# Splitting the expert weights to half precision inside the attention loop, with reordered last tile and interleaved expert blocks

## Chip, cores and metric

One core of one Trainium2 chip. The metric is the device time of one launch in microseconds (us), the median of the runs shown. The core has five instruction streams that run beside each other and meet at semaphores: TensorE (PE, with its weight loads PEld), VectorE (DVE), ScalarE (ACT), GpSimd (POOL) and SyncE (SP, which issues most DMAs). The DMAs of all streams share 16 DMA engines.

## What is computed

A graph attention layer over 4096 rows of width 512, then a mixture of 8 experts with the best two for each row. Both add to their input.

```python
def _L0_gnn_ref(query, key, value, adj_matrix, Wq, bq, Wk, bk, Wv, bv, Wm, bm):
    ...
    scores = jnp.einsum('nd,md->nm', q, k) / scale
    adj_scores = scores * adj_matrix
    adj_scores = jnp.where(jnp.abs(adj_scores) < 1e-05, -1000000000.0, adj_scores)
    prob = jax.nn.softmax(adj_scores, axis=-1)
    x = jnp.einsum('nm,md->nd', prob, v)
    return x @ Wm.T + bm
def _L0_ffn_ref(x, Wg, bg, We, be):
    ...
    gate = jax.nn.softmax(x @ Wg + bg, axis=-1)
    topk_vals, topk_idx = jax.lax.top_k(gate, TOP_K)
    ...
    y = jnp.einsum('bsi,eoi->bseo', x, We) + be[None, None, :, :].transpose(0, 1, 2, 3)
    out = jnp.einsum('bseo,bse->bso', y, gate_sparse)
    return out
x = x + _L0_gnn_ref(_layernorm(x, axis=-1), key, value, adj, ...)
x = x + _L0_ffn_ref(_layernorm(x, axis=-1)[None], Wg, bg, We, be)[0]
```

## The kernel before

**Halves of a number.** A product in single precision is made of half-precision ones: each operand is split into a high half (the value rounded to 16 bits, made by ACT) and a low half (what is left, made by DVE), and PE does three matmuls of 128x512 for each 128-deep piece: high by high, high by low, low by high. The helper `product` (L1276) holds these lines (L1280 to L1282), for the scores as for the experts.

**Set-up.** The weights are folded, then queries, keys and values are projected. The keys' and the values' halves stay on chip (`key_region`, `val_region`). The queries' halves go to DRAM (`q_scratch`) and come back one tile of 128 rows at a time into `q_in`, which has one buffer.

**Attention.** 32 tiles (T) of 128 rows, each in 8 chunks (C) of 512 columns. Below, t is the tile whose scores are being made. PE (`attend`, L1400) makes the scores of chunk c (12 matmuls into one of 4 PSUM banks) and, two chunks behind, multiplies the probabilities of tile t-1 by the values (`times_values`, L1372, 12 matmuls into the bank `o_bank`); chunks 6 and 7 of a tile's values come at the start of the next tile. DVE (`attend`, L1142) multiplies a chunk of scores by the adjacency (`times_adj`, L967, which frees its PSUM bank and the adjacency buffer), ACT takes the absolute value (L737), DVE masks and reduces to a maximum (`mask`, L974, L977). After the tile's eighth chunk ACT makes the exponents twice (L745, L750) and DVE their low halves (`low_half`, L989). SP turns each chunk's halves with a DMA transpose (`turn_probs`, L474) into one of four buffers `pT`.

**Routing, inside the same loop.** For tile t-2, DVE adds the residual (L1009), makes the statistics, normalises (L1032), and, from the gate's logits, finds the two best experts and their weights (`route_top2`, `route_gates`, L1055 to L1077, between the mask of chunk 6 and `times_adj` of chunk 7) with one small exponent by ACT in their middle (`gap_exponent`, L784). `route_slots` (L1083 to L1089) gives each row its two places in a DRAM table sorted by expert (`slots`, one table for each half of the rows, 16 tiles each). POOL (L627, L630) scatters the rows into it, one DMA after the other, and then computes the next tile's deviation (L618).

**SP's order** in a tile is written out by hand in `attend_io` (L482) and decides when each DMA is issued: it waits in place for each condition. Its end matters here:

```python
                for c in range(ADJ, C):
                    turn_probs(t - 1, c)
                    if not last:
                        adjacency(t + 1, c - ADJ)
                    if c == 4 and h is not None:
                        turn_rows(t - 2)
                if not last:
                    sp.wait_ge(s_mm, t * C + C)
                    settle()
                    sp.dma_start(q_in, q_dram[t + 1]).then_inc(q_loaded, 16)
```

**Experts' weights.** When the last tile's scores are done, `key_region` is free. Experts' weights come from DRAM in single precision, 1 MB each, through two buffers `we_in` (L527, L532, L796), and are split in halves of an expert by ACT (`expert_hi`, L798, 128x1024) and DVE (`expert_lo`, L1197), 8 of these 16 pieces while the last tile's values are multiplied and 8 among the first expert blocks. The biases (`be`, 2 MB as broadcast) are one DMA of SP (L537).

**Expert blocks.** A half's table has 39 blocks of 128 rows, most real, the last two or three of each half only padding. The 78 blocks run in order, first all of half 0, then all of half 1. Block s is loaded by SP (`load_block`, L547, 8 buffers), turned by PE (`turn_block`, L1430, two blocks ahead), split by ACT (L815) and DVE (L1232), multiplied by PE (12 matmuls), given its bias by DVE (L1240) and its gate weight by ACT (L822), and added into the output by a POOL DMA (L662). `add_block` (L649) waits for the add four blocks back, and, where an expert's run of blocks begins and for each padding block, for all earlier adds to land. Before half 1's blocks can be loaded, SP pads the table's regions (`pad_regions(1)`, L505 to L511) after block 22, and needs the last tile's routing (`route_slots(T - 1)`, `tables(1)`, L1083 to L1133, on DVE after block 9) and POOL's scatters of it.

## Time and profile before

| | |
|---|---|
| runs | 1905.70, 1904.28, 1902.39 us; median 1904.28 us |
| profiled execution | 1899.79 us, of which the instructions span 1898.1 us |
| PE busy | 1817.8 us, 96% of the span |
| DVE, ACT, POOL busy | 1176.2, 730.1, 239.4 us |
| mean granted TensorE clock | 0.981 |
| DMA | 279.67 MB, mean 147 GB/s |
| set-up, attention, experts | about 0 to 245, 245 to 1600, 1600 to 1898 us |

The busy time of PE tells that it is the bound over most of the span. Where something else sets the time is read from what PE waited for and from the chain of work, stage by stage. A start in the rows is in us from the span's start, and the number behind it is the duration. A bracket at a row's end is the engine's idle time before the instruction and what ended it.

### The profile page before, as it was taken

To read this page: it belongs to the slowest core of one execution; us is meant where nothing else is said; L and a number is where in the kernel's file an instruction comes from. 1 tells how busy PE (TensorE), PEld (TensorE's weight loads), DVE (VectorE), ACT (ScalarE), POOL (GpSimd) and SP (SyncE) were. 2 spreads that over 40 slices of the span, in tenths; PEclk is the share of its full clock that TensorE was granted. 3 is DMA by queue.
4 is the path that set the end of the run, shared out by engine and by line. 5 is a ranking of instruction groups with operands and counts; after the bars stand their busy time and mean duration, and the time that the engine had idled before them with its cause. 6 is when DMAs were issued, how large, how long until landed. Compare 5 with 4: busy or idle time off the path is not lost.

```text
span 1898.1 us, 32739 instructions
## 1 busy us (share of the span) xinstructions
PE 1817.8 (96%) x8730; PEld 851.0 (45%) x8731; DVE 1176.2 (62%) x3056; ACT 730.1 (38%) x1381; POOL 239.4 (13%) x277
## 2 busy tenths in 40 slices
PE   8999999999999999999999999999999996789994
PEld 4544444444444444444444444444444443345552
DVE  2788766666666666666666666666666664634542
ACT  1444444443333344433333344433333442433341
POOL 1000000100000000000000000000000010444454
PEclk9999999999999999999999999999999998899997
DMA  5355455555555555555556555555555558788785
GB/s 200 111 177 188 172 136 124 140 142 137 139 138 133 133 133 145 137 142 134 139 128 176 135 135 144 134 145 133 138 133 136 134 137 244 180 194 165 162 161 78
DMA packets 410860, 279.67 MB, mean 147 GB/s; under 512 B 316737, under 2 KB 316737, under 8 KB 410690
## 3 DMA queue, kind: packets, MB, share of 16 engines
q1 hardware_dynamic: 390914, 234.55, 47.8%
q0 software_dynamic: 16736, 38.35, 10.2%
q10 hardware_dynamic: 3168, 6.29, 1.0%
q8 instruction: 16, 0.26, 0.1%
q14 instruction: 26, 0.21, 0.0%
HBM read 144.29 MB, written 59.33 MB: 107 GB/s over the span
## 4 chain that ended last, share of the span: by engine, by line
PE 75%; DVE 8%; DMA 7%; issue 5%; SPq 2%; ACT 2%; DVEq 0%; POOLq 0%; POOL 0%; ACTq 0%
PE ps L1280 16%; PE ps L1282 16%; PE ps L1281 16%; PE ps L1380 8%; PE ps L1381 8%; PE ps L1382 8%; DMA work<-q_scratch 4%; DVE work L967 2%; PE ps L1289 2%; PE ps L1430 1%; ACT work L737 1%; DMA work<-in_WeT 1%; DMA work<-work 1%; PE ps L1327 1%; DVE work L974 1%
## 5 line engine op out<-in xcount | busy, mean ns | idle before, releaser
L1280 PE MATMUL ps<-key_region,work 128*128 128x512 f16 (+1 forms) x1336 | 509.9, 382 | 9.8 <-DMA work<-q_scratch 7.0
L1281 PE MATMUL ps<-key_region,work 128*128 128x512 f16 (+1 forms) x1336 | 509.4, 381 | 0.0
L1282 PE MATMUL ps<-key_region,work 128*128 128x512 f16 (+1 forms) x1336 | 509.2, 381 | 0.0
L1380 PE MATMUL ps<-val_region,work 128*128 128x512 f16 x1024 | 389.6, 380 | 16.3 <-DMA work<-work 11.4
L737 ACT ACTIVATE work<-work 128x512 f32<-128x512 f32 x256 | 161.3, 630 | 597.2 <-DVE work L967 597.1
L1382 PE MATMUL ps<-val_region,work 128*128 128x512 f16 x1024 | 389.6, 380 | 0.0
L1381 PE MATMUL ps<-val_region,work 128*128 128x512 f16 x1024 | 389.5, 380 | 0.0
L967 DVE SCALAR_TENSOR_TENSOR work<-ps,r_cur,work 128x512 f32<-128x512 f32 x256 | 191.8, 749 | 179.0 <-PE ps L1282 163.3
L989 DVE TENSOR_TENSOR work<-work 128x512 f16<-128x512 f32 x256 | 176.4, 689 | 84.0 <-ACT work L750 83.1
L977 DVE CUSTOM_DVE_ANT_0 work<-work 128x512 f32<-128x512 f32 x256 | 177.3, 693 | 51.2 <-DVE work L974 51.0
L1280 PEld LDWEIGHTS ps<-key_region,work 128*128 128x128 f16 x1336 | 131.2, 98 | 172.9 <-issue 28.8
L745 ACT ACTIVATE work<-work,exp_bias 128x512 f32<-128x512 f32 x256 | 181.4, 708 | 65.6 <-DVE exp_bias L985 61.5
L1282 PEld LDWEIGHTS ps<-key_region,work 128*128 128x128 f16 x1336 | 131.4, 98 | 158.8 <-issue 3.4
L1281 PEld LDWEIGHTS ps<-key_region,work 128*128 128x128 f16 x1336 | 131.3, 98 | 148.0 <-issue 3.0
L750 ACT ACTIVATE work<-work,exp_bias 128x512 f16<-128x512 f32 x256 | 180.7, 706 | 0.0
L974 DVE TENSOR_SCALAR work<-work 128x512 f32<-128x512 f32 x256 | 109.2, 426 | 113.2 <-ACT work L737 109.2
L1380 PEld LDWEIGHTS ps<-val_region,work 128*128 128x128 f16 x1024 | 100.2, 98 | 131.8 <-DMA work<-work 12.0
L1382 PEld LDWEIGHTS ps<-val_region,work 128*128 128x128 f16 x1024 | 100.4, 98 | 122.0 <-issue 1.9
L1381 PEld LDWEIGHTS ps<-val_region,work 128*128 128x128 f16 x1024 | 100.4, 98 | 114.0 <-issue 1.5
L662 POOL DMA_INDIRECT out<-val_region,tok_ids x78 | 123.9, 1588 | 152.7 <-DMA out<-val_region,tok_ids 66.6
L627 POOL COPY work<-gate 128x1 f32<-128x1 f32 x64 | 14.6, 228 | 856.9 <-DVE slots_u L1089 776.6
L822 ACT ACTIVATE val_region<-work,tok_gates 128x512 f32<-128x512 f32 x78 | 56.3, 722 | 160.6 <-DVE work L1240 138.8
(149 smaller groups left out, 1542.9 us busy)
## 6 DMA issues: line engine op xcount, KB each, us to landing
work<-in_adj SPq DMA_DIRECT2D x256, 256.0 KB, 2.8
work<-slots SPq DMA_DIRECT2D x40, 257.0 KB
val_region<-slots SPq DMA_DIRECT2D x38, 257.0 KB
work<-in_valueT SPq DMA_DIRECT2D x8, 1024.0 KB, 6.8
work<-in_x SPq DMA_DIRECT2D x8, 1024.0 KB, 5.0
work<-in_keyT SPq DMA_DIRECT2D x8, 1024.0 KB, 5.4
q_scratch<-work SPq DMA_DIRECT2D x8, 1024.0 KB, 5.0
work<-q_scratch SPq DMA_DIRECT2D x32, 256.0 KB, 3.0
```

The costliest lines, as they stand in the source:

```text
L737: nc.scalar.activation(w[:, c * CW:(c + 1) * CW], s_adj[:, c % 2, :], ACT.Abs).then_inc(abs_done, 1)
L745: nc.scalar.activation(prob[:, c % 2, :], w[:, c * CW:(c + 1) * CW], ACT.Exp, bias=exp_bias[:, :], scale=1.0 / SS, accum_out=sum_part[:, c ...
L750: nc.scalar.activation(p_split[:, c, 0:CW], w[:, c * CW:(c + 1) * CW], ACT.Exp, bias=exp_bias[:, :], scale=1.0 / SS).then_inc(p_hi, 1)
L967: nc.vector.scalar_tensor_tensor(s_adj[:, c % 2, :], s_bank(c), r_cur[:, :], adj_in[:, c % ADJ, :], ALU.add, ALU.mult).then_inc(s_read, 1)
L977: nc.vector.tensor_tensor_reduce(out=masked, in0=s_adj[:, c % 2, :], in1=masked, scale=1.0, scalar=-3.0e38, op0=ALU.add, op1=ALU.max, accu ...
L989: nc.vector.tensor_tensor(p_split[:, c, CW:2 * CW], prob[:, c % 2, :], p_split[:, c, 0:CW], ALU.subtract).then_inc(p_lo, 1)
L1280: nc.tensor.matmul(bank, st[0], mv[0], start=(k == 0), stop=False)
L1281: nc.tensor.matmul(bank, st[0], mv[1], start=False, stop=False)
L1282: last = nc.tensor.matmul(bank, st[1], mv[0], start=False, stop=(k == n - 1))
L1380: nc.tensor.matmul(o_bank, st[0], mv[0], start=first, stop=False)
L1381: nc.tensor.matmul(o_bank, st[0], mv[1], start=False, stop=False)
L1382: last = nc.tensor.matmul(o_bank, st[1], mv[0], start=False, stop=final)
```

## The change

**Weights.** In the attention tiles 2 to 17 (the 16 tiles with h == 0), each tile splits a sixteenth of the experts' weights in four pieces of 128x256 values: SP loads a piece (128 KB, rows of 1 KB) into `we_stage`, ACT makes the high half, DVE the low half, and SP stores both (rows of 512 B) in a DRAM scratch `we_halves`. There is one buffer for a piece and one for its halves, so the load of a piece waits for DVE's use of the one before it, and ACT's high half waits for the store of the one before it to have landed. After the last scores ACT issues the loads of the ready halves: experts 0 and 1 at once, expert 2 after the fourth exponent chunk, the other five and all biases (now eight DMAs of 256 KB) after the last exponent. `expert_hi` and `expert_lo` go. SP's `expert_ready` counts experts for PE.

**Last tile.** PE runs its scores in front of most of the values of the tile before (`attend_last`), and its own values go to another PSUM bank (`o_last`), so that they don't wait for the residual of the tile before.

**Blocks.** The first 15 blocks are of half 0; then 48 alternate between the halves; the last 15 are of half 1. Tok buffers go from 8 to 16. The last tile's gate logits come after block 3 (before: 5), its ranks after 6 (8), its slots and tables after 7 (9), its scatters after adds 6 and 8 (10 and 13). The padding of half 1's regions is issued by ACT after block 9, no longer by SP after block 22.

```diff
-    EARLY = 23
-    LATE = 7
+    LEAD = 15
+    AHEAD = 2
+    TOKS = 16
...
-        we = key_region[:, :].rearrange("p (h e k o) -> p h e k o", h=2, e=E, k=KC)
+        we = key_region[:, :].rearrange("p (e h k o) -> p e h k o", h=2, e=E, k=KC)
...
+        we_stage = q1_words[:, 0:WP]
+        we_halves = q1_words[:, WP:2 * WP].bitcast(F16).rearrange("p (h o) -> p h o", h=2)
...
-        weT_v = WeT.rearrange("e (k p) o -> e p k o", p=P)
+        weT_parts = WeT.rearrange("e (a k p) (c o) -> (e a) p k c o", a=2, p=P, c=2)
+        we_dram = nc.dram_tensor("we_halves", (2 * E, P, 2, 2 * D), F16, kind="Internal").ap()
...
+            def __init__(self, first, turn=0, later=False):
+                self.first, self.turn, self.later = first, turn, later
+                middle = LEAD <= first < SEQ - LEAD
+                self.h = (first - LEAD) % 2 if middle else int(first >= LEAD)
+                if middle:
+                    k = (first - LEAD) // 2 + (0 if self.h else LEAD)
+                else:
+                    k = first if first < LEAD else first - BLOCKS
+                at = k + self.h * BLOCKS
+                self.at = at if is0(turn) else at + turn * (TURN // 2)
...
+            def split_piece(i, q):
+
+                if not (is0(i) and q == 0):
+                    sp.wait_ge(piece_lo, i * PIECES + q)
+                settle()
+                sp.dma_start(we_stage, weT_parts[i, :, q // 2, q % 2, :]).then_inc(piece_loaded, 16)
+
+            def store_piece(i, q):
+
+                sp.wait_ge(piece_lo, i * PIECES + q + 1)
+                settle()
+                sp.dma_start(we_dram[i, :, :, q * WP:(q + 1) * WP], we_halves).then_inc(piece_stored, 16)
+
...
+                splits = h == 0
+                if splits:
+                    split_piece(t - 2, 0)
                 turn_probs(t - 1, 0)
                 turn_probs(t - 1, 1)
...
+                if splits:
+                    store_piece(t - 2, 0)
+                    split_piece(t - 2, 1)
                 if h is not None:
...
+                    if splits and c in (5, 6, 7):
+                        store_piece(t - 2, c - 4)
+                        if c < 7:
+                            split_piece(t - 2, c - 3)
                 if not last:
                     sp.wait_ge(s_mm, t * C + C)
                     settle()
                     sp.dma_start(q_in, q_dram[t + 1]).then_inc(q_loaded, 16)
...
-            sp.wait_ge(s_read, T * C)
-            sp.dma_start(we_in[0], weT_v[0]).then_inc(we_loaded[0], 16)
-            for c in range(4):
...
+            for c in range(5):
...
+                if c == 3:
+                    residual_io(T - 2, 1)
...
+            def expert_ready(e):
+
+                sp.wait_ge(we_loaded[e], 48)
+                sp.sem_inc(we_ready, 1)
...
+            for e in range(2, E):
+                expert_ready(e)
+            sp.wait_ge(slotted, 32 * T)
+            sp.wait_ge(padded[1], 16 * E)
+            for st in turn_steps(0):
+                load_block(st)
...
+            def piece_high(i, q):
+                act.wait_ge(piece_loaded, i * (PIECES * 16) + (q + 1) * 16)
+                if not (is0(i) and q == 0):
+                    act.wait_ge(piece_stored, i * (PIECES * 16) + q * 16)
+                nc.scalar.activation(we_halves[:, 0, :], we_stage, ACT.Copy, scale=WS).then_inc(piece_hi, 1)
...
+                    if splits:
+                        piece_high(t - 2, c - 2)
                 if routes:
                     split_rows(t - 2)
                 for c in range(4, 7):
                     absolute(t, c)
+                    if splits and c > 4:
+                        piece_high(t - 2, c - 3)
...
+            def load_expert(e):
+                for a in range(2):
+                    nc.scalar.dma_start(we[:, e, :, 2 * a:2 * a + 2, :].rearrange("p h k o -> p h (k o)"),
+                                        we_dram[2 * e + a]).then_inc(we_loaded[e], 16)
+
+            def load_bias(e):
+                nc.scalar.dma_start(be_all[:, e, :], be[e:e + 1, :].to_broadcast([P, D])).then_inc(we_loaded[e], 16)
+
+            act.wait_ge(piece_stored, 16 * PIECES * 2 * E)
+            act.wait_ge(s_mm, T * C)
+            load_expert(0)
+            load_expert(1)
             for c in range(C):
                 exponent(T - 1, c)
...
+            act.wait_ge(p_hi, T * C)
+            for e in range(3):
+                load_bias(e)
+            for e in range(3, E):
+                load_expert(e)
+                load_bias(e)
...
+                if st.first == 9:
+                    act.wait_ge(tables_done, 2)
+                    for e in range(E):
+                        at = act.value_load(pad_at[0:1, 1, e:e + 1], min_val=0, max_val=(DUMMY - 1) * P)
+                        nc.scalar.dma_start(slots[1][bass.ds(at, P), :], pad_row[:, :]).then_inc(padded[1], 16)
...
+            def piece_low(i, q):
+                dve.wait_ge(piece_hi, i * PIECES + q + 1)
+                nc.vector.scalar_tensor_tensor(we_halves[:, 1, :], we_stage, WS, we_halves[:, 0, :],
+                                               ALU.mult, ALU.subtract).then_inc(piece_lo, 1)
...
                 times_adj(t, 3)
+                if splits:
+                    piece_low(t - 2, 0)
...
                 mask(t, 4)
+                if splits:
+                    piece_low(t - 2, 1)
                 times_adj(t, 5)
                 mask(t, 5)
+                if splits:
+                    piece_low(t - 2, 2)
...
                 times_adj(t, 6)
                 mask(t, 6)
                 if h is not None:
                     route_top2(t - 2)
                     route_gates(t - 2)
+                if splits:
+                    piece_low(t - 2, 3)
                 times_adj(t, 7)
...
-                if c == 0 and not is0(t):
+                if c == 0 and isl(t, T):
+                    pe.wait_ge(s_read, T * C)
+                elif c == 0 and not is0(t):
                     pe.wait_ge(x1_done, t)
...
+            def attend_last():
+
+                t = T - 1
+                scores(t, 0)
+                scores(t, 1)
+                for c in range(C - LAG, C):
+                    times_values(t - 2, c)
+                for c in range(2, 6):
+                    scores(t, c)
+                times_values(t - 1, 0)
+                scores(t, 6)
+                times_values(t - 1, 1)
+                gate_logits(t - 2)
+                scores(t, 7)
+                for c in range(2, C):
+                    times_values(t - 1, c)
+                    if c == 4:
+                        ranks(t - 2)
+
```

## Rows read from the trace of the kernel before

**Rows 1.** Stretches: length, PE, PEld, DVE, ACT, POOL busy, clock, DMA share, GB/s.
```profile
688.00:730.00 42.00, 41.77 (x204) 18.91 (x202) 27.04 (x74) 16.36 (x35) 3.04 (x5) 1.00 0.54 136
1560.00:1602.00 42.00, 28.35 (x126) 12.56 (x125) 21.91 (x52) 16.57 (x26) 4.11 (x5) 0.84 0.93 255
...
1700.00:1866.00 166.00, 166.00 (x876) 89.81 (x875) 81.31 (x216) 65.06 (x108) 77.28 (x51) 1.00 0.84 164
```

**Rows 2.** What PE waited for, whole run: us in total, times, longest.
```profile
PE ps L1280 <- DMA work<-q_scratch: 7.0, 23, 0.5
```

**Rows 3.** PE in order of time, its starts after idle time, from 1576 us.
```profile
1576.27 0.39 PE L1380 MATMUL ps<-val_region,work 128*128 128x512 f16 x1 [2.97 <-DMA work<-work]
1589.05 0.61 PE L1380 MATMUL ps<-val_region,work 128*128 128x512 f16 x1 [8.46 <-DMA work<-work]
1601.52 0.39 PE L1280 MATMUL ps<-key_region,work 128*128 x1 [0.41 <-issue]
...
1658.99 0.68 PE L1430 MATMUL ps<-ident,val_region 128*128 128x128 f32 x4 [2.83 <-DVE work L1232]
```

**Rows 4.** DVE in order of time in one attention tile, chunks 6 and 7.
```profile
657.34 0.75 DVE L967 SCALAR_TENSOR_TENSOR work<-ps,r_cur,work 128x512 f32<-128x512 f32 x1 [2.33 <-PE ps L1282]
...
663.38 0.75 DVE L967 SCALAR_TENSOR_TENSOR work<-ps,r_cur,work 128x512 f32<-128x512 f32 x1 [0.20 <-DVE picked L1077]
```

**Rows 5.** ACT in the same tile, the routing's exponent.
```profile
661.72 0.20 ACT L784 ACTIVATE egap<-gap 128x1 f32<-128x1 f32 x1 [2.89 <-DVE gap L1065]
```

**Rows 6.** SP's DMA issues in the same tile, in order of time.
```profile
653.14 0.34 SPq L465 DMA_DIRECT2D work<-in_adj  x1
...
658.32 0.33 SPq L465 DMA_DIRECT2D work<-in_adj  x1
...
664.36 0.34 SPq L465 DMA_DIRECT2D work<-in_adj  x1
665.02 0.33 SPq L503 DMA_DIRECT2D work<-q_scratch  x1
```

**Rows 7.** PE at the start of the next tile.
```profile
668.20 0.39 PE L1280 MATMUL ps<-key_region,work 128*128 128x512 f16 x1 [0.29 <-DMA work<-q_scratch]
```

**Rows 8.** Line L465, 250 to 1000 us, its DMAs of 256 KB.
```profile
DMA to landing us min/median/max: 2.6/2.8/4.0
```

**Rows 9.** DVE's groups, 1550 to 1660 us: count, busy us, mean ns, idle before.
```profile
L1197 DVE SCALAR_TENSOR_TENSOR key_region<-work,key_region 128x1024 f16<-128x1024 f32 x16 | 19.6, 1223 | 15.7 <-ACT key_region L798 15.6
```

**Rows 10.** ACT's groups in the same stretch, same columns.
```profile
L798 ACT ACTIVATE key_region<-work 128x1024 f16<-128x1024 f32 x16 | 16.5, 1045 | 17.8 <-DMA work<-in_WeT 13.2 <-DVE key_region L1197 4.6
...
L737 ACT ACTIVATE work<-work 128x512 f32<-128x512 f32 x1 | 0.6, 630 | 2.2 <-DVE work L967 2.2
```

**Rows 11.** POOL in order of time: a tile's first gate copy, the next deviation.
```profile
1555.58 0.18 POOL L627 COPY work<-gate 128x1 f32<-128x1 f32 x1 [25.07 <-DVE slots_u L1089]
...
1567.93 0.57 POOL L618 TENSOR_TENSOR rstd<-var_eps,neg_half 128x1 f32<-128x1 f32 x1 [4.11 <-DMA slots<-work,slots_u]
```

**Rows 12.** DMA queues, 1585 to 1587 us: packets, MB, share of 16 engines.
```profile
q10 hardware_dynamic: 309, 0.63, 87.6%
q1 hardware_dynamic: 316, 0.08, 18.1%
```

**Rows 13.** DMA queues, 1561 to 1563 us, transposes alone on SP's queue.
```profile
q1 hardware_dynamic: 1703, 0.43, 111.5%
```

**Rows 14.** Line L474, transposes issued from 1577 to 1590 us.
```profile
DMA to landing us min/median/max: 9.6/9.6/9.6
```

**Rows 15.** ACT's gate of expert block 3, in order of time.
```profile
1626.12 0.72 ACT L822 ACTIVATE val_region<-work,tok_gates 128x512 f32<-128x512 f32 x1 [2.13 <-DVE work L1240]
```

**Rows 16.** The gates of blocks 21 to 77: count, duration, first and last start.
```profile
L822 ACT ACTIVATE val_region<-work,tok_gates x57: 721/722/723, 1703.0 to 1871.6; 128x512 f32<-128x512 f32 x57
```

**Rows 17.** SP's padding of half 1's regions.
```profile
1681.56 11.26 SPq L511 DMA_DIRECT2D slots<-pad_row  x8
```

**Rows 18.** POOL's last add in order of time.
```profile
1890.45 1.54 POOL L662 DMA_INDIRECT out<-val_region,tok_ids  x1 [4.06 <-DMA out<-val_region,tok_ids]
```

291 lines of the change are left out of this document (124 added, 167 removed).

## The prediction

> **What bounds the kernel now.** I read the stretches first. In a steady attention tile PE is busy 41.77 of 42 us at full clock, while DVE and ACT have 15 and 25 us to spare [rows 1]. So the added splitting has room as busy time; what matters is whether it lies on a chain that ends in a PE wait. Then the waits: in the attention loop PE waits for one thing only, the load of the next tile's queries, 23 times, 0.3 us each [rows 2]. So that load is already the last to be ready: its chain has no slack, and each us put on it is a us of the tile.
>
> The chain, read in one tile. DVE takes chunk 6's scores at 657.34, goes through the mask and the routing's small steps, and takes chunk 7's at 663.38, without idling but for ACT's exponent at 661.72 [rows 4, 5]. Chunk 7's `times_adj` lets SP issue the adjacency load (664.36), and only behind it the query load (665.02) [rows 6]. PE starts at 668.20 after 0.29 us of idle time [rows 7]. The scores of chunk 7 had long been made: it is DVE's routing and SP's order that hold the load back.
>
> The second place is the end of attention: from 1560 to 1602 PE is busy 28.35 of 42 us at a mean clock of 0.84 [rows 1], with waits for transposed probabilities of 2.97 and 8.46 us, and the first expert product is at 1601.52 [rows 3]. Third, the blocks from 3 to 21: their gates are at 1626.1 and 1703.0, 76.9 us for 18 blocks, where blocks 21 to 77 take 168.6 us for 56, 3.0 each [rows 15, 16]. From 1700 on PE is never idle [rows 1], and the last add is issued 18.1 us after the last gate has ended (1890.45 against 1872.3) [rows 16, 18].
>
> **The change in the attention loop (16 tiles).** Added for a tile: four loads and four stores on SP, four ACT and four DVE operations. By size, an ACT high half costs about 0.4 us (1045 ns for 1024 columns, 630 for 512) [rows 10], a DVE low half 0.4 to 0.5 (1223 ns for 1024, 750 for 512) [rows 4, 9]. Six of the eight lie in idle time. Pieces 0 and 1 delay the routing's rows at most, which aren't needed for some us. Piece 2 stands in front of `times_adj` of chunk 6: its load can be issued at 653.14 + 2 x 0.6 = 654.3, the 0.6 being SP's spacing of two issues [rows 6]. If it lands 2.3 us later, the two halves are done at 657.4: 0.1 us late against 657.34. Piece 3 lies on the chain in three ways:
> - SP can issue store 2 and load 3 only after the adjacency load of 658.32, so at 658.9 and 659.5. Landed at 661.8 and split by ACT at 662.2, it holds up `gap_exponent`, which stands behind it on ACT and ran at 661.72: 0.5 us.
> - DVE's low half of piece 3, between the gates and `times_adj` of chunk 7: 0.4 us.
> - SP's store of piece 3, in front of the query load: 0.6 us, and 0.1 for the load behind it on the queue.
>
> Sum with piece 2: 1.7 us a tile, 27 us for 16. The landing of 128 KB isn't in the trace. Rows of 256 KB land after 2.8 (2.6 at least) [rows 8], and half the bytes should take less, so I take 2.3. If it is 2.8 with a slow store, pieces 2 and 3 each wait 0.5 us more: 2.8 a tile, 45 us. If both waits vanish, 1.0 stays (DVE 0.4, SP 0.6): 16 us. A gain is excluded, since nothing is taken from the loop. The gaps of 2 us a tile should not lower the clock: it stayed at 1.00 with the present ones.
>
> The Trainium skill (DMA: Bandwidth & Descriptors, "Anatomy of one DMA — SWDGE (gpsimd) path") fits a DMA at 2.0 us plus bytes over 436 GB/s, for another issuing path. It gives 2.6 us for 256 KB, where the median here is 2.8 [rows 8], and 2.3 us for 128 KB; by it a tile costs the same 1.7 us.
>
> **The last tile.** With four score chunks in front, DVE is no longer fed by PE in the second half of the tile but limited by its own 2.85 us a chunk, and the last exponents start some 3 us earlier. The 1.8 us wait for the residual's bank goes. But the scatter chain of POOL stays: a tile's gate copy to the next deviation takes 12.35 us [rows 11], its start moves by 1.5 us only, and the row split of tile 30 stands in front of ACT's last exponent, which so ends at about 1569.6. Right then ACT issues 5 experts and 8 biases, 5 x 512 + 8 x 128 = 3584 packets of 2 KB. SP's last three transposes, of 1024 packets of 256 B each (256 KB a chunk), meet them. Alone, transposes move 850 packets a us (1703 in 2 us) [rows 13]; next to a weight load both queues get equal numbers, some 155 a us each (316 and 309 in 2 us) [rows 12]. So each takes 1024 / 158 = 6.5 us: they land at about 1578, 1585 and 1592, where the rows of before have 9.6 us from issue to landing [rows 14]. The blocks' rows are queued behind them. PE's chunk 5 starts at 1579 (before 1589), but chunk 7 ends at about 1599 at a half clock: the first expert product at about 1600, against 1601.5. Here the burst takes back what the reordering gives.
>
> **The first blocks.** No split stands any more between the blocks. Blocks 0 to 2 don't wait (the deviation of tile 31 comes at 1590.5 + 0.7 + 12.35 = 1603.5, in the time of the third product). Block 3 starts at 1609, its gate at 1612.5 against 1626.1: 14 us gained. The weights themselves are there: the burst ends at about 1594.
>
> From there to block 21: 18 x 3.0 = 54 us, plus stalls. DVE's slots and tables after block 7 cost what they do now, 2.8 us [rows 3]. The padding moves to ACT: 8 issues with a register load each, 11.3 us on SP [rows 17]; behind it on ACT stands the high half of block 12, and PE has two blocks of 3 us in hand: 9 us of idle time (6 to 11). Then block 15's rows, which SP loads only after that padding: 2.3. The half clock after such a gap, 3; small ones 1.5. Sum 54.2 + 18.6 = 72.8, against 76.9: 4 us gained, and the stall that SP's padding caused has only moved to another engine. In all 18 to 19 us by block 21.
>
> From block 21 PE's rate is the same, and so is the number of adds that wait for all earlier ones (7 changes of expert in each half and 5 padding blocks), if in another order. The end stays 18 us behind the last gate. So the tail gains 19 us. Bounds: 11 (padding at its dearest, transposes later) to 33; above that POOL limits, whose 78 adds with their waits need some 250 us from the first one.
>
> **Sum.** 27 - 19 = 8 us slower: 1899.8 + 8 = 1907.8 for the profiled execution, which lies 4.5 below the median of the runs; 1904.3 + 8 = 1912.
>
> **The rivals.**
> - *The tail pays for it all* (ends faster). The place is the burst against the transposes. If ACT's loads don't share the engines evenly with them, they land 4 us after issue, PE multiplies chunks 5 to 7 without a gap at full clock and the blocks start near 1587: up to 33 us gained (then POOL limits). With 1.2 us a tile (19 us), 1904 - 14 = 1890. It decides from where the tail's gain exceeds 16 times the tile's added time. For it: the splits did cost 1.3 us a block. Against it: the equal packet counts [rows 12]. Chance 0.27, 1884 to 1900.
> - *Both cancel*, 22 against 20: 1901 to 1908. Chance 0.14.
> - *The piece's round trip is slow*: small store packets make the landing 3 us, and pieces 2 and 3 both hold up DVE: 45 - 17 = 28 slower, 1932. Chance 0.09. For it: the longest landings are 4.0 [rows 8]. Against it: the queue is empty at these moments.
> - *The change doesn't do what it says*: the ready halves arrive no sooner than the old ones, since PE's first blocks were held by routing and POOL. Then the tail gains 4 and the loop costs 27: 1927. Inside the forecast's range; against it stands the 4.3 us a block of blocks 0 to 3, which ends with the splits.
> - *Forecast*: 1908 to 1930, chance 0.50 with the one before.
>
> A measurement of this kernel tells about 0.2% (3.8 us) from no change. Faster 0.27, same 0.14, slower 0.50 + 0.09 = 0.59. Range: 19 - 33 = 14 faster to 45 - 15 = 30 slower, 1890 to 1934.
>
> **What would show it.** In the loop of tiles 2 to 17 PE's wait for `q_scratch` should be near 2.0 us a tile (0.3 now), and back at 0.3 from tile 18; the exponent of L784 should follow piece 3's high half; SP should have the store between L465 and L503. At the end: three transposes with about 6.5 us between their landings; the first expert product near 1600 + 27; block 3's gate some 14 us earlier by this count; an idle PE of 6 to 11 us behind ACT's padding. The prediction is wrong if PE's query wait stays under 1 us a tile, or if the first product comes 10 us sooner than said.

## The result

| | before | after |
|---|---|---|
| median of 4 runs | 1904.0 us | 1967.1 us (1956.7 to 1969.5) |
| profiled execution | 1899.8 | 1969.5 |
| PE busy | 1817.8 | 1837.5 |
| mean granted clock | 0.981 | 0.973 |

The changed kernel is slower, ratio 1.032 [1.028, 1.036]. The forecast had the sign and the places, 1912 us and 1934 at most. It missed two sizes: in the two profiled executions the loop lost 71 us, not 27, and the tail gave nothing, not 19. (By the medians the whole difference is 63 us: the profiled execution of the changed kernel is its slowest run, that of before is faster than its runs.)

To place the time I split both traces at SP's last query load (start of the last tile). From the first to the 18th query load: 719.1 us before, 789.7 after, 70.6 more. From the 18th to the last: 505.8 and 506.4. From the last to the end of the span: 387.5 and 387.2. So everything was lost in tiles 2 to 17, and the tail came out even. It is 381.1 to 384.3 us in `e2`, `e3` and `e4` below, whose tails have the same code, so some 3 to 6 us of gain may be there that this execution doesn't show; 19 aren't in any.

Busy time first: from 284 to 1030 us (lengths as in [rows 1]). With the same code for scores and values, PE is busy for 693 of 746 us; before it was 738.6.

```profile
284.00:1030.00 746.00, 693.09 (x3251) 307.69 (x3249) 455.17 (x1247) 285.99 (x609) 46.76 (x76) 0.98 0.60 146
```

PE's waits from 330 to 1080 us in the changed kernel (total, times, longest), against 0.3 us a tile before [rows 2]:

```profile
PE ps L1323 <- DMA work<-q_scratch: 53.8, 17, 3.5
```

One tile's end, read as [rows 4 to 7] were, engine by engine (start, duration, idle time before and what ended it). L488 loads a piece, L494 stores its halves, L785 is ACT's high half, L1189 VectorE's low half, L1012 `times_adj`, L527 the query load.

```profile
642.57 0.34 SPq L466 DMA_DIRECT2D work<-in_adj  x1
643.24 0.59 SPq L494 DMA_DIRECT2D we_halves<-work  x1
644.09 0.38 SPq L488 DMA_DIRECT2D work<-in_WeT  x1
...
649.30 0.59 SPq L494 DMA_DIRECT2D we_halves<-work  x1
650.16 0.38 SPq L488 DMA_DIRECT2D work<-in_WeT  x1
...
656.24 0.34 SPq L466 DMA_DIRECT2D work<-in_adj  x1
656.91 0.59 SPq L494 DMA_DIRECT2D we_halves<-work  x1
657.84 0.34 SPq L527 DMA_DIRECT2D work<-q_scratch  x1
```
```profile
646.73 0.42 ACT L785 ACTIVATE work<-work 128x256 f16<-128x256 f32 x1 [3.66 <-DMA work<-in_WeT]
...
653.03 0.42 ACT L785 ACTIVATE work<-work 128x256 f16<-128x256 f32 x1 [4.03 <-DMA work<-in_WeT]
653.36 0.19 ACT L818 ACTIVATE egap<-gap 128x1 f32<-128x1 f32 x1
```
```profile
647.52 0.74 DVE L1012 SCALAR_TENSOR_TENSOR work<-ps,r_cur,work 128x512 f32<-128x512 f32 x1
...
653.65 0.15 DVE L1116 TENSOR_SCALAR den<-egap 128x1 f32<-128x1 f32 x1 [1.79 <-ACT egap L818]
...
655.26 0.74 DVE L1012 SCALAR_TENSOR_TENSOR work<-ps,r_cur,work 128x512 f32<-128x512 f32 x1
```
```profile
660.90 0.39 PE L1323 MATMUL ps<-key_region,work 128*128 128x512 f16 x1 [3.23 <-DMA work<-q_scratch]
...
661.91 0.63 PE L1324 MATMUL ps<-key_region,work 128*128 128x512 f16 x1
```

Read it upward from PE: it waits 3.23 us for the query load, which SP issues 1.60 us behind the adjacency load (0.66 in [rows 6]) because the store of piece 3 stands between. That adjacency load waits for DVE at 655.26, DVE for ACT's exponent, and the exponent stands behind ACT's high half of piece 3, for which ACT had been idle 4.03 us. All four engines wait in turn for one transfer of 128 KB.

The last line is the second loss. A matmul that takes 0.38 us at full clock takes 0.63 from 661.6 on: 3.4 us at half clock (1.2 GHz), right behind the gap. Two periods side by side (columns of [rows 1]), the first with such a stretch, the second without:

```profile
657.84:704.77 46.93, 43.69 (x202) 19.28 (x202) 28.41 (x79) 17.85 (x38) 3.04 (x5) 0.96 0.62 145
704.77:750.10 45.33, 42.04 (x202) 18.87 (x202) 28.38 (x79) 17.86 (x38) 3.19 (x5) 1.00 0.62 150
```

Ten of the 16 split tiles' periods (from one query load to the next) hold one and are 47.2 us long; the others are 45.4 but for the first, 46.7. Before they were 42.1. So 16 x 3.3 us for the chain and 10 x 1.7 for the clock (3.4 us at half clock do the work of 1.7): 70 us. Counted by waits it is 16 for the queries, of 3.15 to 3.5 us each, and 11 have a half-clock stretch behind them, the eleventh just past the split tiles.

**The tail.** Marks in us behind the last query load (gates by their ends), one profiled execution of each kernel (before, after, forecast for after):

| | before | after | forecast |
|---|---|---|---|
| gap exponent of tile T-2 | 73.6 | 89.5 | - |
| gate of block 0 | 102.9 | 107.3 | 94 |
| gate of block 3 | 116.2 | 117.4 | 103 |
| gate of block 21 | 193.1 | 190.0 | 174 |
| last gate | 361.7 | 358.6 | 343 |
| end of span | 387.5 | 387.2 | 369 |

ACT in order of time at the end of attention:

```profile
1644.54 0.71 ACT L774 ACTIVATE work<-work,exp_bias 128x512 f16<-128x512 f32 x1
1645.28 2.81 ACTq L832 DMA_DIRECT2D work<-in_be  x3
...
1655.42 4.73 ACTq L832 DMA_DIRECT2D work<-in_be  x1
...
1669.76 0.20 ACT L818 ACTIVATE egap<-gap 128x1 f32<-128x1 f32 x1 [24.51 <-issue]
```

and PE's waits there, 1580 to 1960 us:

```profile
PE ps L1497 <- DVE work L1277: 13.0, 3, 6.6
PE ps L1443 <- DVE picked L1122: 9.2, 1, 9.2
PE ps L1426 <- DMA work<-work: 8.5, 4, 5.0
```

ACT needs 24.5 us to issue 18 DMAs (7 MB), single ones up to 4.73. The exponent of tile T-2's gate stands behind them, and PE waits 9.2 us for the ranks (L1443). That is this execution's share: in `e4` the same run takes 20.0 us and PE waits 1.1 for the ranks. The 6.6 us are the wait behind ACT's padding; the forecast had 9 (6 to 11).

A second delay lies ahead of that run. POOL's scatter chain for tile T-3, from a gate's copy to the next deviation, took 12.35 us before [rows 11]. It starts 1.5 us sooner now, as forecast, but takes 18.3, for the first scatter lands late (POOL, changed kernel):

```profile
1623.79 0.18 POOL L654 COPY work<-gate 128x1 f32<-128x1 f32 x1 [21.78 <-DVE slots_u L1134]
1636.23 0.18 POOL L654 COPY work<-gate 128x1 f32<-128x1 f32 x1 [10.20 <-DMA slots<-work,slots_u]
1642.12 0.57 POOL L645 TENSOR_TENSOR rstd<-var_eps,neg_half 128x1 f32<-128x1 f32 x1 [3.90 <-DMA slots<-work,slots_u]
```

The loads of experts 0 to 2 are issued from 1617.9 to 1626.5, around it. The row split and the last exponent hang on this deviation: the exponent ends 65.0 us behind the query load, where the forecast had 59.0.

### The profile page after: what moved, and what is told of

Same layout as the page of the kernel before. It is cut to its first block, busy times and chain, and to the rows that moved or that the text cites. A ratio compares the mean times of both kernels' runs of the same rounds, so it can differ in the third digit from the quotient of the medians.

```text
span 1967.5 us, 33715 instructions
## 1 busy us (share of the span) xinstructions
PE 1837.5 (93%) x8730; PEld 853.1 (43%) x8731; DVE 1179.7 (60%) x3104; ACT 736.1 (37%) x1429; POOL 235.5 (12%) x277
## 4 chain that ended last, share of the span: by engine, by line
PE 65%; DMA 14%; DVE 7%; issue 6%; SPq 4%; ACTq 2%; ACT 2%; POOLq 1%; DVEq 0%; POOL 0%
PE ps L1323 14%; PE ps L1325 14%; PE ps L1324 14%; PE ps L1426 6%; PE ps L1427 6%; PE ps L1428 6%; DMA work<-in_WeT 4%; DMA work<-q_scratch 4%; DMA out<-val_region,tok_ids 4%; DVE work L1012 3%; SPq L494 2%; PE ps L1332 1%; SPq L466 1%; PE ps L1497 1%; DMA slots<-work,slots_u 1%
## 5 line engine op out<-in xcount | busy, mean ns | idle before, releaser
L1323 PE MATMUL ps<-key_region,work 128*128 128x512 f16 (+1 forms) x1336 | 516.6, 387 | 59.4 <-DMA work<-q_scratch 57.1
L1324 PE MATMUL ps<-key_region,work 128*128 128x512 f16 (+1 forms) x1336 | 515.5, 386 | 0.0
L1325 PE MATMUL ps<-key_region,work 128*128 128x512 f16 (+1 forms) x1336 | 515.4, 386 | 0.0
L1012 DVE SCALAR_TENSOR_TENSOR work<-ps,r_cur,work 128x512 f32<-128x512 f32 x256 | 191.6, 749 | 161.9 <-PE ps L1325 153.1
L1323 PEld LDWEIGHTS ps<-key_region,work 128*128 128x128 f16 x1336 | 132.5, 99 | 225.5 <-issue 84.0
L1325 PEld LDWEIGHTS ps<-key_region,work 128*128 128x128 f16 x1336 | 132.8, 99 | 163.5 <-issue 11.0
L1324 PEld LDWEIGHTS ps<-key_region,work 128*128 128x128 f16 x1336 | 132.7, 99 | 151.6 <-issue 9.8
```

What stands on the lines that cost most here:

```text
L1012: nc.vector.scalar_tensor_tensor(s_adj[:, c % 2, :], s_bank(c), r_cur[:, :], adj_in[:, c % ADJ, :], ALU.add, ALU.mult).then_inc(s_read, 1)
L1323: nc.tensor.matmul(bank, st[0], mv[0], start=(k == 0), stop=False)
L1324: nc.tensor.matmul(bank, st[0], mv[1], start=False, stop=False)
L1325: last = nc.tensor.matmul(bank, st[1], mv[0], start=False, stop=(k == n - 1))
```

## The experiments

Theory A: the loop's loss is order, not traffic; pieces stand in front of what the query load waits for, and the gap then lowers the clock. Rival B: the 8 MB loaded and 8 MB stored burden the queues. Each kernel's edit is against the changed kernel, or the one it names; "off the chain" is `e4`.

**The pieces out, and their order.** `e1b`, on SP, ACT and DVE:

```diff
-                splits = h == 0
+                splits = False
...
-                                        we_dram[2 * e + a]).then_inc(we_loaded[e], 16)
+                                        q_dram[4 * e + 2 * a:4 * e + 2 * a + 2].rearrange("t p f -> p t f")).then_inc(we_loaded[e], 16)
```

> Leaves out the whole split in the loop (no piece is loaded, halved or stored); everything of the tail stays, and the experts' 16 loads, of the same size and packets, read the query scratch instead, so the expert products are of other numbers. Theory A, all the loss is the pieces in 16 tiles of the loop and the tail is worth nothing: the period of tiles 2 to 17 is back at 42.1 us from 46.7, and the time is that of the kernel before, 1899 to 1909 us. Rival B, the tail itself gained as predicted but lost it again to something that the pieces leave behind (a late piece store, the scratch's reads): then without pieces the tail's gain shows, 1885 to 1895. Rival C, something else of the change costs in the loop (a longer program, other buffers): above 1915.

Measured 1893.9 us, ratio 0.994 [0.992, 0.996]. The period is back at 42.1 us (theory A's part), but the time is 9 us below before, inside rival B's range: the tail is worth 5.6 us here (381.9 from the last query load to the end). Rival B's reason doesn't hold, for `e2` to `e4`, with all pieces, have nearly the same tail (381.1 to 384.3).

`e2`, on ACT:

```diff
-                    if splits and c > 4:
-                        piece_high(t - 2, c - 3)
+                    if splits and c == 5:
+                        piece_high(t - 2, 2)
                 if routes:
                     gap_exponent(t - 2)
+                if splits:
+                    piece_high(t - 2, 3)
                 absolute(t, 7)
```

> Only ACT's order at the end of a tile: the gap exponent ahead of the fourth piece's high half. Theory A (the tile's chain is ACT's wait for the piece, then the exponent, then VectorE's gate work, then the low half, then the last multiplication): the exponent leaves the wait, the low half comes about 1.2 us earlier, PE's wait a tile goes from 3.2 to about 2.0 us, and with it the 3.4 us at half clock: 16 x 1.2 + 19 = 38 us less, about 1929; 1948 if the half-clock stretches stay. Rival B (the pieces' transfers load the queues and the memory, and order is nothing): 1962 to 1970.

Measured 1932.9, ratio 1.015: theory A, if 4 us short (the wait went to 2.4 us, not 2.0, and not all half-clock stretches went). `e3`, on SP:

```diff
                     sp.dma_start(q_in, q_dram[t + 1]).then_inc(q_loaded, 16)
+                if splits:
+                    store_piece(t - 2, 3)
```

> Only SP's order: the store of the fourth piece behind the next tile's query load. Theory A: the query load is issued 0.94 us earlier, PE's wait is 2.3 us instead of 3.2; 15 us less with the half-clock stretches kept (1952), 34 less if a gap of 2.3 us no longer brings them (1933). Rival B (transfers, not order): 1962 to 1970.

Measured 1940.7 (1936.4 to 1944.8), ratio 1.020, between theory A's two numbers. `e4` is both, and on DVE:

```diff
-                if splits:
-                    piece_low(t - 2, 2)
                 times_adj(t, 6)
+                if splits:
+                    piece_low(t - 2, 2)
```

and the same for piece 3 and `times_adj(t, 7)`.

> Both of those, and VectorE's low halves of pieces 3 and 4 behind the multiplications of chunks 6 and 7 instead of ahead of them. The same pieces, transfers and instructions, none of them ahead of anything that the query load waits for. Theory A: period of a tile back at 42.1 to 42.4 us, PE waiting 0.3 to 0.6 us a tile, no half-clock stretch in the loop: 1897 to 1910. Rival B (16 MB through the queues cost by themselves): 1940 or more. Rival D (the gap is the ends' sum, but the fourth piece now ends in the next tile and delays its first piece): 1915 to 1935.

Measured 1900.6, ratio 0.999 [0.998, 1.000]. PE's waits from 330 to 1080 us, `e2`, `e3`, `e4`:

```profile
PE ps L1325 <- DMA work<-q_scratch: 38.3, 17, 2.9
```
```profile
PE ps L1324 <- DMA work<-q_scratch: 40.6, 17, 2.7
```
```profile
PE ps L1326 <- DMA work<-q_scratch: 6.9, 16, 0.6
```

Rival B falls: `e4` moves every byte of the changed kernel, and its period is 41.9 to 42.7 us (48.9 in the one tile where the loop program changes; 45.1 before). The half clock goes with the gap's length. Of the 16 waits for the queries 11 have a stretch of it behind them in the changed kernel (waits of 3.15 to 3.5 us), 3 in `e2` (2.1 to 2.9), 2 in `e3` (2.2 to 2.7) and none in `e4` (0.2 to 0.6). One more stretch in `e2` and one in `e4` stand behind waits of 2.1 and 4.2 us for the residual, in the tile where the loop program changes; in that tile the kernel before waits 3.04 us and stays at full clock. Which gap brings one isn't settled, only that fewer do when they are shorter.

**The tail, ACT's run of loads.** `gap_exponent(T - 2)` goes ahead of the biases and experts 3 to 7, in `e6` on `e4`, in `e12` on the changed kernel:

```diff
             act.wait_ge(p_hi, T * C)
+            gap_exponent(T - 2)
             for e in range(3):
                 load_bias(e)
             for e in range(3, E):
                 load_expert(e)
                 load_bias(e)
-            gap_exponent(T - 2)
```

> The changed kernel with one edit: the gap exponent of tile T-2 ahead of ACT's run of biases and experts 3 to 7. In its profile that run held the exponent for 24.5 us and PE waited 9.2 us for the ranks behind it. Theory A: the wait goes, and of it 4 to 9 us reach the end: 1957 to 1963, ratio to the kernel before 1.028 to 1.031. Rival B (the wait only takes the place of others, for the end hangs on the last tile's rows): 1964 to 1969, ratio 1.032 to 1.034.

Measured 1960.1, ratio 1.030 [1.028, 1.033]: theory A's range, though the interval overlaps that of the changed kernel, so the times alone hardly tell. In the trace the 9.2 us wait is gone and the tail is 378.0 us instead of 387.2. But ACT's run still stands ahead of the high halves of the first blocks' rows, and PE now waits for those, 11.0 us instead of 3.7 (PE's waits, 1580 to 1960 us):

```profile
PE ps L1497 <- DVE work L1277: 21.8, 3, 11.0
```

The same wait is 9.4 us in `e6` and 11.9 in `e8`. Moving one instruction out from behind the run hands the wait to the next one behind it.

> On the kernel with the pieces off the chain (1900.6 us): the gap exponent of tile T-2 ahead of ACT's run of biases and experts 3 to 7, which held it for 20.0 us. Theory A (the hold is what the last tiles' gating loses, but PE has block products to fill it): rank wait 1.1 us gone, POOL's scatter no longer ahead of the last tile's reciprocal root (3.3 us); 1 to 4 us less, 1896 to 1900. Rival B (the end hangs on this gating, and 20 us of it come back): 1885 to 1892. Rival C (nothing in the tail waits for it any more): 1899 to 1902.

Measured 1895.4, ratio 0.996 [0.994, 0.997]: just past theory A's range. `e9`, on `e4`, asks what the run is:

```diff
-                    nc.scalar.dma_start(we[:, e, :, 2 * a:2 * a + 2, :].rearrange("p h k o -> p h (k o)"),
-                                        we_dram[2 * e + a]).then_inc(we_loaded[e], 16)
+                    nc.scalar.dma_start(we[:, e, 0:1, 2 * a:2 * a + 2, :].rearrange("p h k o -> p h (k o)"),
+                                        we_dram[2 * e + a, :, 0:1, :]).then_inc(we_loaded[e], 16)
```

> On the kernel with the pieces off the chain: each of the 16 loads of expert weights brings only the high halves (the low halves stay whatever lies there), so the products are of other numbers. It asks what ACT's 20 us between the last exponential and the gap exponent are. Theory A, the queue is full and each issue waits for bytes to leave (8 MB in 16 loads): with half the bytes the run takes about half, 8 to 12 us. Rival B, a fixed price of an issue, 1.1 us each: 18 to 20 us still. Neither moves the time by over 4 us from 1900.6.

ACT's run took 14.7 us, between both: 2.5 of 7 MB less took 5.3 off 20.0; at that rate 7 MB are 14.8 us, which leaves some 5 for 18 issues. So a good part of each issue is bytes that have to leave first. The second half of my expectation was wrong: the time fell to 1890.3, for the first gate came at 95.9 instead of 102.0. `e9` also tells what made POOL's chain long. With half the bytes in the loads of experts 0 to 2 it takes 13.0 us, near the 12.35 of before; with all of them it takes 15.2 to 18.7 in every version. POOL in `e9`:

```profile
1557.17 0.18 POOL L655 COPY work<-gate 128x1 f32<-128x1 f32 x1 [21.78 <-DVE slots_u L1137]
1563.82 0.18 POOL L655 COPY work<-gate 128x1 f32<-128x1 f32 x1 [4.40 <-DMA slots<-work,slots_u]
1570.14 0.57 POOL L646 TENSOR_TENSOR rstd<-var_eps,neg_half 128x1 f32<-128x1 f32 x1 [4.33 <-DMA slots<-work,slots_u]
```

**What sets the end.** `e7` takes the eight padding stores from ACT to SP, ahead of its wait for the last rows; `e8` is `e6` and `e7`:

```diff
-                if st.first == 9:
-                    act.wait_ge(tables_done, 2)
...
+            pad_regions(1)
             sp.wait_ge(slotted, 32 * T)
             sp.wait_ge(padded[1], 16 * E)
             for st in turn_steps(0):
```

> On the kernel with the pieces off the chain: the eight padding stores of the second half from SP, in its wait for the last rows, instead of from ACT between blocks 9 and 10. In that kernel ACT issues nothing else for 12.3 us there, PE waits 7.3 us behind it, and 10.2 us at half clock follow. Theory A (that stall is real): 7.3 us and some 3 to 5 us of half clock back, 1888 to 1893. Rival B (PE, without it, runs into block 15, whose rows are loaded at 1666.8 us only, and waits there instead): 1896 to 1901.

> Both together: pieces off the chain, gap exponent ahead of the loads, padding on SP. Theory A, sum of the parts: 1885 to 1891. Rival B (the end of the tail is set by the rows of the last tile, whatever comes before): 1896 to 1900.

Measured 1899.4 and 1894.9: rival B in `e7`, neither in `e8` (the time of `e6`). PE's two longest waits in `e4` (first fence) and in `e7` (second):

```profile
PE ps L1500 <- DVE work L1280: 11.2, 3, 7.3
PE ps L1429 <- DMA work<-work: 8.7, 4, 5.3
```
```profile
PE ps L1425 <- DMA work<-work: 12.5, 4, 5.4
PE ps L1496 <- DMA val_region<-slots: 8.9, 2, 8.1
```

The stall behind ACT became a stall for block 15's rows (L1496). Block 15 is the first that SP loads behind its waits for the last tile's scatters and for the padding. Next, the weights later: `e10` issues experts 5 to 7 behind ACT's halves of the first two blocks, `e11` experts 3 to 7 one by one in its steps of blocks 0 to 4, `e13` in those of blocks 4 to 8; `e15` is `e13` with the padding on SP. In `e13`:

```diff
                 if st.first == 4:
                     gap_exponent(T - 1)
+                if 4 <= st.first < 9:
+                    load_expert(st.first - 1)
+                    load_bias(st.first - 1)
```

(In `e11`, `e13`, `e15` and `e14` a routing that needs a late expert in the first blocks would stall.)

> On the kernel with the pieces off the chain and the gap exponent early (1895.4 us): experts 5 to 7 are loaded by ACT behind the halves of the first two blocks' rows, not ahead of the first block. Halving the bytes brought the first expert gate from 102.0 to 95.9 us behind the last query load, and the time by 10 us. Theory A (the first rows of the blocks, and the last tile's own transposed scores, share the queues with 8 MB of weights): with 3 MB of them later the first gate comes at 96 to 99 us and the time is 1888 to 1893. Rival B (the burst only moves: ACT is held for 7 us at blocks 2 and 3): 1894 to 1898. Rival C (what halving saved was the memory's time as a whole): 1893 to 1896.

> The same, but experts 3 to 7 one at a time in ACT's steps of blocks 0 to 4 (an order that these numbers of tokens allow; a routing that needed expert 3 or later in the first blocks would stall it for good). Theory A: no burst is left, first gate at 95 to 98 us, ACT's hold of 18 to 20 us gone: 1886 to 1891. Rival B (each issue of 0.5 MB now delays a block on ACT by some 2 us, PE waits for the rows' halves): 1893 to 1900.

Measured 1895.4 and 1894.0, rival B's and C's numbers. In `e10` the first gate came at 97.8 us, as theory A had it, in `e11` at 87.9, 14 sooner than in `e4`, and the end hardly moved. In `e11` the turned rows of the last tile are what PE stood for:

```profile
1603.13 1.57 SPq L481 DMA_TRANSPOSE work<-work  x1
```
```profile
1621.33 0.38 PE L1439 MATMUL ps<-wg_split,work 128*128 128x16 f16 x8 [12.30 <-DMA work<-work]
```

This transposed load took 18.2 us to land among 3 MB of weights; in `e4`, with the weights ahead of it, 6.6, and in `e13`, with them behind it, 4.6 (but 4.6 too in `e16` below, where they are ahead of it as in `e4`, so that small difference isn't theirs).

> As the kernel with the loads spread over blocks 0 to 4 (1894.0 us), but experts 3 to 7 in ACT's steps of blocks 4 to 8, behind the transposed load of the last tile's rows. In that kernel this load was issued at 1603.1 and PE waited 12.3 us for it, until 1621.3, with 3 MB of weights issued between 1601.1 and 1608.5; in the kernel with the weights ahead of it it took 6.7 us. Theory A (the end hangs on the last tile's gating, and this on a transposed load that shares the queues with the weights): the wait falls to 0 to 3 us, everything behind comes 9 to 12 us earlier, 1880 to 1887. Rival B (the next stall, ACT's eight padding stores or the rows of block 15, takes it): 1889 to 1894.

> That, with the eight padding stores on SP. Theory A: another 3 to 7 us, for the last tile's rows now come early enough that block 15 no longer waits: 1875 to 1883. Rival B (block 15 follows the scatters of the last tile by its own chain of some 30 us and waits as before, 8 to 9 us): the same as with the padding on ACT, within 2 us.

Measured 1895.3 and 1898.5: the 12.3 us wait is gone, as theory A said, and the times are nearest to rival B's (`e15` is 3 us slower than `e13`, not within 2). In `e15` one long wait is left:

```profile
1653.38 10.09 SPq L535 DMA_DIRECT2D slots<-pad_row  x8
1668.83 0.35 SPq L563 DMA_DIRECT2D val_region<-slots  x1
```
```profile
1671.46 1.12 PE L1496 MATMUL ps<-ident,val_region 128*128 128x128 f32 x4 [17.73 <-DMA val_region<-slots]
```

The padding takes 10.1 us to issue, and block 15 is loaded 5.4 us behind it. It needs the last tile's tables, but these were made here at 1641.9, 11.5 us before it began (DVE's last table, then SP's longest waits from 1600 to 1680 us):

```profile
1641.76 0.16 DVE L1177 TENSOR_SCALAR tab_expert<-tab_f 1x39 uint32<-1x39 f32 x1
```
```profile
SPq L568 <- DMA work<-in_be: 28.9, 5, 7.3
```

L568 is `expert_ready`: SP stood there until the late loads of expert 7 had landed (1652.5), with the padding behind it in its order. In `e7` and `e8`, where the weights come early, SP's padding starts 0.7 and 0.8 us behind the tables. So most of the 17.7 us comes of joining late weights with padding on SP, and `e15` is no test of how late the last tile's rows are. `e14` is `e15` with the lead of before, and `e17` is `e8` with it, `e16` is `e4` with it (in all three SP also loads blocks 16 to 22 behind its waits for the experts):

```diff
-    LEAD = 15
+    LEAD = 23
```

> That, with a lead of 23 blocks of the first half instead of 15, so that PE has 8 blocks more, 24 us of products, before it needs a row of the last tiles. Theory A (the rows of the last tile are late, and the change's shorter lead is what shows it): PE's waits for slots' rows go, 1868 to 1878. Rival B (23 blocks of one half at the end make the adds to one half follow each other: the end comes 3 us or more later behind the last gate): 1878 to 1885. Rival C (no wait was left there): the same as with a lead of 15 within 2 us.

> On the kernel with pieces off the chain, gap exponent early and padding on SP, weights in one run as in the changed kernel (1894.9 us): the lead of 23. There PE waits 9.0 us for rows of block 15 and 10 us at half clock follow. Theory A: both go, 1881 to 1887, about the time of the kernel with late weights and a lead of 23 (1883.6), so that it's the lead and not the place of the weights that pays. Rival B (the weights' place pays by itself): 1888 to 1893.

> On the kernel with the pieces off the chain (1900.6 us): the lead of 23 blocks of the first half instead of 15, nothing else (SP waits for the experts' loads behind row load 16, so as not to stand still ahead of them). Theory A (with a lead of 15, block 15 cannot begin before the last tile's rows are loaded, 164 to 168 us behind the last query load in every kernel so far, though block 0's gate lay between 88 and 107; a longer lead fills that time with products): PE's wait for rows is gone, but ACT's padding still holds it: 1888 to 1896. Rival B (the lead only pays where ACT's burst and padding are mended too, for in this kernel PE reaches block 15 no sooner than its rows): 1899 to 1902.

Measured 1883.6 (0.989 [0.986, 0.992]), 1886.3 (0.991 [0.988, 0.993]) and 1897.0 (0.996). `e14` took rival B's time, but not by its mechanism: its end comes 27.7 us behind the last gate, 26.5 in `e15`. What keeps it from theory A's is 5.5 us that PE still waits for rows (17.7 in `e15`): SP issues the padding only at 1662.5, 19.5 us behind the tables. `e17` is theory A: the lead pays without the late weights. `e16` lies between A and B, and its trace shows no gain (382.2 us from the last query load to the end, 381.1 in `e4`): PE still waits 6.4 us behind ACT's padding (7.3 in `e4`), as rival B's reason has it. The marks behind the last query load:

| | gate 0 | gate 15 | last gate | end |
|---|---|---|---|---|
| before | 102.9 | 164.6 | 361.7 | 387.5 |
| after | 107.3 | 172.0 | 358.6 | 387.2 |
| `e4` off the chain | 102.0 | 165.8 | 352.4 | 381.1 |
| `e7` padding on SP | 104.0 | 170.8 | 357.3 | 382.7 |
| `e8` | 100.0 | 164.3 | 351.7 | 378.7 |
| `e11` weights in blocks 0 to 4 | 87.9 | 163.8 | 350.5 | 378.2 |
| `e13` weights in blocks 4 to 8 | 90.1 | 163.3 | 350.6 | 378.3 |
| `e15` and padding on SP | 91.6 | 167.6 | 355.0 | 381.5 |
| `e16` = `e4`, lead 23 | 104.3 | 165.3 | 353.1 | 382.2 |
| `e17` = `e8`, lead 23 | 100.6 | 153.1 | 339.9 | 367.6 |
| `e14` = `e15`, lead 23 | 91.2 | 149.0 | 341.6 | 369.3 |

With a lead of 15 the gate of block 15 comes 64 to 67 us behind the gate of block 0 in every version but `e11`, `e13` and `e15`, where it is 73 to 76. So an earlier start is carried through to block 15 as a rule, and these three lose it on the way: `e11` by the wait for the transposed load, `e13` and `e15` between the gates of blocks 3 and 7 (21.1 and 18.1 us, 15.2 in `e4`; that ACT's issues of weights in these steps are the cause is argued, not tested), `e15` by SP's wait besides. Behind block 15 all go alike: 186 to 187 us to the last gate, 25 to 29 more to the end.

## Why the prediction was right and wrong

**Right.** The place and the sign of the loop's loss: PE's wait for the queries was the chain without slack, and all three parts of piece 3 and the one of piece 2 are in the trace. From tile 18 on nothing changed. The last exponents start 3.5 us earlier (I said 3). From block 3 on the tail went as forecast: 72.6 us from its gate to that of block 21 (I said 72.8), with 6.6 us of PE's idle time behind ACT's padding (I said 9, 6 to 11) and 1.6 for block 15's rows (2.3), and from there 168.6 to the last gate, as before.

**Wrong: "27 us for 16".** The mechanism stood, its terms were small. In the tile shown they are 0.75 us for piece 2 (0.1 predicted), 1.46 for the exponent behind piece 3 (0.5), 0.34 for DVE (0.4), 0.94 for SP (0.7): 3.5 a tile for 1.7, and that tile's period is 3.6 longer. The common cause is the round trip: I took SP's spacing of two issues as 0.6 us from rows of plain loads; the store follows the adjacency load by 0.67 and the piece's load the store by 0.86, the store alone 0.59 of issuing for 0.34. And I took 2.3 us of landing, below the lowest row (2.6), by the argument that half the bytes take less. It was 2.6:

```profile
DMA to landing us min/median/max: 2.1/2.6/3.1
```

Both errors count twice, for pieces 2 and 3 (piece 3's load took 2.9 us in the tile shown, from 650.16 to ACT's start at 653.03). The rival "the piece's round trip is slow", 45 us, was nearest, and had 0.09. Its sum is itself a little off: 1.7 + 2 x 0.5 is 2.7 a tile and 43 us.

The Trainium skill (DMA: Bandwidth & Descriptors, "Anatomy of one DMA — SWDGE (gpsimd) path") gave 2.3 us for 128 KB by its fit, which is for another issuing path; the measured median is 2.6. For 256 KB it gave 2.6, and the adjacency loads of the changed kernel have a median of 2.9. Both lie 0.3 above it.

**Wrong: "the gaps of 2 us a tile should not lower the clock".** It stayed at 1.00 with gaps of 0.3, which says nothing of gaps ten times as long. At 3.3 us 10 of the 16 periods had 3.4 us at half clock, 17 us in all. The trace of before had the warning: its clock of 0.84 at the end of attention [rows 1] stands beside waits of 2.97 and 8.46 us [rows 3]. It also had one wait of 3.04 us, near 980 us, without any half clock, so a chance and not a certainty was to be read from it. The Trainium skill (TensorE: Matmul & The Clock Gate, "HAM oscillation — how this bites in real kernels") tells of a wait for data in every turn of a loop that costs the clock every time; here 11 of the 16 waits did, and 5 did not.

**Wrong: the tail, 19 us.** Of the 18 us that are missing at the end 14 were lost before the gate of block 3, which came at 117.4 us and not at 103. Three terms failed. (1) ACT's 18 issues were costed for what they do to the transposes, not for ACT: 24.5 us, with the exponent of tile T-2 and the high halves of the first blocks' rows behind them. PE waited 9.2 us for the one and 3.7 for the other; in `e12`, with the exponent out of the way, 11.0 for the other. Of a step that is moved to an engine I had left out who stands behind it there. Only where the run itself leaves the first blocks (`e11`, `e13`) does block 0's gate come at 88 to 90 us, where I had 94. (2) I took POOL's scatter chain as 12.35 us, as before. It took 18.3 among the loads of experts 0 to 2 and 13.0 with half their bytes (`e9`). The last exponent so ended 6.0 us later than I said, and the last transposed chunk landed at 85.5 instead of 81.4. (3) The end lies 28.6 us behind the last gate and not 26, as I took from before; no run was made for this, and its cause stays open.

The shorter lead was not a missing term: its price, the 9 us behind the padding and the 2.3 for block 15's rows, stood in the forecast. But I called the new order's adds equal and did not ask what a lead of 23 had been worth. With the padding on SP it gives 8.6 us (`e8` to `e17`). The 14.8 us from `e15` to `e14` hold the stall that `e15` makes for itself.

The range was narrow too. Its slow end took 45 us for the loop and a gain of 15 in the tail; with my own lower bound for the tail, 11, it would have been 1938. The loop alone put the time outside either.

The rival "the tail pays for it all" (0.27) had as its condition that the transposes land 4 us after issue. The last three took 8.3, 11.0 and 16.1 us. In `e12` the last two took 3.4 and 3.3, and the first product still came at 94.0 us behind the query load, not near 76: the condition alone would not have been enough. "The ready halves arrive no sooner" was nearest in the tail's size, and partly in its reason: PE was held by the routing of tile T-2, but behind ACT's issues, which that rival doesn't name.

## What to carry to other kernels

Work put into an engine's idle time is free only if it stands behind, in each queue, what the next wait hangs on: here the same 16 MB cost 71 us in front of it and 6 behind it (from the first to the 18th query load 725.3 us in `e4`, 719.2 in `e1b`; 3.9 of the 6 fall in the one tile where the loop program changes). A hand-written order has to be read queue by queue, and a wait for a round trip of a transfer counts in each queue behind it. When an instruction is moved out from behind a long run of issues, look for the next one behind the same run (`e12`), and when a step is moved to another engine, for what that engine waits for first (`e15`). A shorter lead gives up work that hid a wait. The two fastest versions, `e14` and `e17`, 1.1% and 1.0% below the kernel before, keep the change's pieces and take its lead back.

## What the hardware showed

- A wait of 3.15 to 3.5 us of PE was followed by 3.4 us at half clock (1.2 GHz) in 11 of 16 cases, one of 2.1 to 2.9 us in 3 of 16 (`e2`) and 2 of 16 (`e3`), one of 0.2 to 0.6 us in none (`e4`).
- Issuing a DMA holds its engine when many bytes are under way: 18 issues took 24.5 us (20.0 in `e4`, 14.7 with 4.5 MB for 7), one of them 4.73. The Trainium skill (DMA: Bandwidth & Descriptors, "Issuing engines are not separate DMA queues") calls an engine's time to initiate usually small beside the transfer; here it was 24.5 of the 34.6 us from the first issue to the last landing.
- A strided store of 512 B rows takes 0.59 us to issue, plain loads 0.34.
- One transposed load landed after 4.6 to 6.6 us in most versions and after 18.2 us with 3 MB of weight loads issued around it (`e11`). That equal packet counts decide this [rows 12] fits, but no run tells it apart from bytes.
- POOL's first scatter of a tile held POOL for 4.0 us in the kernel before, for 6.8 to 10.4 us with the loads of three experts issued around it, and for 4.4 with half their bytes (`e9`).
